# One layer's side work on fixed points: VectorE's long pieces cut and spread, GpSimd's routing first, half of a zero-clearing in the opening

## What is computed

```python
x = x + 0.5 * _L0_ffn_ref(_layernorm(x, axis=-1), ...)      # chain 1
x = x + _L0_attn_ref(_layernorm(x, axis=-1), ...)           # 16 heads of 16 channels
x = x + 0.5 * _L0_ffn_ref(_layernorm(x, axis=-1), ...)      # chain 2
x = x + 0.5 * _L1_ffn_ref(_layernorm(x, axis=-1), ...)      # 32 experts, 4 per token
x = x + _L1_attn_ref(_layernorm(x, axis=-1), ...)
x = x + 0.5 * _L1_ffn_ref(_layernorm(x, axis=-1), ...)
```

## Time and profile before

| | us |
|---|---|
| median of 3 runs | 1552.89 |
| lowest and highest | 1550.59, 1554.79 |
| profiled execution, its own time | 1556.93 |
| its span, first to last instruction | 1555.1 |
| first layer's maxima and scores, first to last start (L389, L400) | 71.6 to 504.3 |

### The profile page before, as it was taken

The page is one execution under the profiler, slowest core; times in us unless marked ns, Lnnn a source line. Parts: engine busy times, 40 slices in busy tenths (PEclk is TensorE's granted clock), DMA queues, the critical chain, the costliest instruction groups (busy, mean ns, idle before and its releaser), DMA issues.

```text
span 1555.1 us, 20966 instructions
## 1 busy us (share of the span) xinstructions
PE 1224.5 (79%) x5960; PEld 751.6 (48%) x5960; DVE 935.5 (60%) x2702; ACT 676.1 (43%) x1706; POOL 547.7 (35%) x558
## 2 busy tenths in 40 slices
PE   4777877887878528999556989889989999299990
PEld 2432333332232316888423546555655656188870
DVE  6777566856754312232359887988788695232227
ACT  2223544554647114555324554455355354155550
POOL 2053270246353134555121121144125133455550
PEclk8786897998989759999779999999999999699995
DMA  4657065092031345554301000020001001444448
GB/s 117 109 93 205 21 88 177 21 164 101 26 138 39 125 165 190 164 160 149 133 13 42 28 28 1 1 79 31 1 11 45 33 33 44 149 160 156 156 136 274
DMA packets 80379, 147.94 MB, mean 95 GB/s; under 512 B 13885, under 2 KB 62078, under 8 KB 77326
## 3 DMA queue, kind: packets, MB, share of 16 engines
q1 hardware_dynamic: 62286, 104.41, 24.0%
q0 software_dynamic: 17408, 42.00, 7.6%
q10 hardware_dynamic: 576, 0.18, 0.0%
HBM read 83.21 MB, written 63.00 MB: 94 GB/s over the span
## 4 chain that ended last, share of the span: by engine, by line
PE 53%; DVE 28%; issue 7%; ACT 6%; DMA 2%; POOL 2%; SPq 1%; another core or an unknown queue 1%; DVEq 0%; POOLq 0%; ACTq 0%
PE m_psG L1057 11%; PE m_psY L1073 5%; DVE a_t L1483 4%; PE a_psO L414 3%; DVE a_mx L758 3%; PE a_psA L1251 3%; PE a_psU L389 3%; DVE a_nb L1491 3%; PE a_psS L400 3%; PE m_psX L1048 3%; PE a_psU L1233 2%; PE a_psT L310 2%; PE a_psU L1239 2%; PE a_psO L1274 2%; ACT a_pr L1354 2%
## 5 line engine op out<-in xcount | busy, mean ns | idle before, releaser
L138 POOL DMA_INDIRECT outs_dram<-m_ys,dest x192 | 184.0, 958 | 165.7 <-ACT m_ys L996 152.8
L1354 ACT ACTIVATE a_pr<-a_psA,a_nb 128x512 f32<-128x512 f32 (+3 forms) x256 | 132.6, 524 | 220.4 <-DVE a_nb L1491 219.5
L758 DVE TENSOR_REDUCE a_mx<-a_psU 128x1 f32<-128x512 f32 x256 | 165.2, 684 | 104.8 <-PE a_psU L389 91.0
L1016 DVE TENSOR_TENSOR m_hm<-m_psG,m_sg 128x128 f32<-128x128 f32 x192 | 55.9, 291 | 282.7 <-ACT m_sg L990 173.6
L1410 POOL TENSOR_TENSOR a_q<-a_q,a_t 64x512 f32<-64x512 f32 x64 | 80.8, 1263 | 358.0 <-DVEq L1486 336.2
L1057 PE MATMUL m_psG<-arena,m_xgT 128*128 x768 | 205.6, 391 | 0.8 <-issue 0.2
L533 ACT ACTIVATE a_P<-a_psS 128x512 f32<-128x512 f32 x256 | 143.6, 597 | 93.6 <-PE a_psS L400 80.2
L138 POOL DMA_INDIRECT rows_dram<-a_xd,slot x128 | 124.7, 974 | 142.5 <-DVE a_xd L124 76.2
L389 PE MATMUL a_psU<-arena 96*128 96x512 bf16 x256 | 108.0, 428 | 45.8 <-DVE a_mx L758 35.3
L1057 PEld LDWEIGHTS m_psG<-arena,m_xgT 128*128 128x128 f32 x768 | 133.5, 194 | 16.1 <-issue 4.0
L1491 DVE TENSOR_REDUCE a_nb<-a_psA 128x1 f32<-128x512 f32 (+3 forms) x256 | 113.2, 484 | 36.8 <-PE a_psA L1253 27.1
(11 more groups left out here) (249 smaller groups left out, 2222.7 us busy)
## 6 DMA issues: line engine op xcount, KB each, us to landing
m_xg<-rows_dram SPq DMA_DIRECT2D x48, 512.0 KB
arena<-in_mo_w SPq DMA_DIRECT2D x9, 2048.0 KB
arena<-part_dram SPq DMA_DIRECT2D x96, 128.0 KB
rows_dram<-arena SPq DMA_DIRECT2D x12, 1024.0 KB, 12.1
arena<-outs_dram SPq DMA_DIRECT2D x16, 512.0 KB, 3.6
part_dram<-a_part SPq DMA_DIRECT2D x16, 384.0 KB
m_xg<-outs_dram SPq DMA_DIRECT2D x8, 512.0 KB, 4.4
m_ys<-outs_dram SPq DMA_DIRECT2D x8, 512.0 KB, 5.0
```

The source lines that it names most:

```text
L138: pool.indirect_dma_start(out=rows_dram, out_offset=bass.IndirectOffsetOnAxis(ap=slot[:, c:c + 1], axis=0), in_=row, in_offset=None).then_ ...
L758: dve.tensor_reduce(mx[g % 2][:, 4 * kt + qt:4 * kt + qt + 1], psU[n % 2][:, :], AX, ALU.max).then_inc(u_free, 1)
L1354: ins = act.activation(pr[S % 2][:, AT[t]:AT[t] + (t + 1) * P], psA[:, AT[t]:AT[t] + (t + 1) * P], ACT.Exp, bias=nb[S % 2][:, t:t + 1], sc ...
```

## The change

- The places are new: `F1` 7 to 20, `F2` 25 to 33 (that is point 1 of the iteration after), scales of the projections at 7 and 11 instead of 0, their rows, transposes and products at 13 to 18 instead of 1 to 8.
- A chain has 19 steps instead of 13: one `gate_row` per point, `gates` in two halves (`GA`, `GB`), and in chain 2 the scales in two pieces (`SB`, `SE`).
- `batch_scales` is cut into `scales_begin` (10 instructions) and `scales_end` (6), at `QSC`, `OSC` and `SB`/`SE`.
- The two additions of the output projection stand at one point.
- `bases` moves behind the first two reductions of iteration 0; `places` from point 0 to point 3 of iteration 1.
- POOL: per iteration `bias`, then all of the routing or the table writes, then `terms`, then all rows.
- Six of the twelve zeroing DMAs are issued in the opening, from a part of the probabilities' buffer (`blank`) that POOL clears first; ACT's first exponential waits for them. The other six stay in iteration 0, and none are left in iteration 1.

```diff
-    F1, F2 = 7, 25
-    QSC, QLN, QT, QK, QV = 0, 1, 2, 3, 7
-    AT, OP, OA, OST, OSC = 19, 20, 21, 23, 24
+    F1, F2 = 20, 33
+    TX, GM, GAP, GA, GB, TH, LM, LA, ST, SB, SE, XD = 1, (2, 3, 4, 5), 6, 7, 8, 9, 10, 11, {1: 12, 2: 13}, 14, 16, 18
+    QSC, QLN, QT, QK, QV = (7, 11), 13, 14, 15, 17
+    AT, OP, OA, OST, OSC = 19, 20, 21, 23, (29, 30)
...
+def scales_end(dve, link, sc):
+
+    root_steps(dve, link, sc.var[:, :], sc.rstd[:, :], sc.tmp[:, :], 2)
...
-    inverse_root(dve, link, sc.var[:, :], sc.rstd[:, :], sc.tmp[:, :])
+    root_guess(dve, link, sc.var[:, :], sc.rstd[:, :], sc.tmp[:, :])
+    root_steps(dve, link, sc.var[:, :], sc.rstd[:, :], sc.tmp[:, :], 1)
...
+                        if st == 0 and c == 0:
+                            act.wait_ge(wiped[0], 16 * 6)
...
-                if i == -1 and p == F1 + 12:
+                if i == 0 and p == 0:
                     dve.tensor_scalar(weight[:, :], weight[:, :], 0.5, None, ALU.mult)
                     bases()
-                if i == 1 and p == 0:
+                if i == 1 and p == 3:
                     places()
...
+            pool.memset(blank, 0.0).then_inc(blanked, 1)
...
-            for i in range(-2, B + 2):
+            for i in range(0, B + 2):
                 b = i + 1
-                if 1 <= b < B:
+                if i == 0:
+                    pool.wait_ge(rest_in, 16 * NREST)
+                if i < B:
+                    bias(i)
+                if i == 0:
+                    for part_of in range(3):
+                        route(part_of)
+                if 1 <= i <= 3:
+                    entry((0, 22, 43)[i - 1], (22, 43, 64)[i - 1])
+                if b < B:
                     for c in range(4):
                         terms(b, c)
...
+                if 0 <= i - 2 < B:
+                    rows(i - 2, 0, TPB * TOPK)
...
+            sp.wait_ge(blanked, 1)
+            clear(0, blank)
```

More of the change, by code:

```diff
@@ L183, in turn_units @@
         out = []
-        if ffn_at(i, p, 1):
-            out += [("x",) + ffn_at(i, p, 1) + (u,) for u in range(2)]
-        if ffn_at(i, p, 7):
-            out.append(("h",) + ffn_at(i, p, 7))
+        if ffn_at(i, p, TX):
+            out += [("x",) + ffn_at(i, p, TX) + (u,) for u in range(2)]
+        if ffn_at(i, p, TH):
+            out.append(("h",) + ffn_at(i, p, TH))
         if p == QT and 0 <= i + 1 < B:
@@ L200, in main_units @@
         out = []
-        for step, js in ((2, (0, 1)), (3, (2,)), (4, (3,))):
+        for j, step in enumerate(GM):
             if ffn_at(i, p, step):
-                out += [("m",) + ffn_at(i, p, step) + (j,) for j in js]
-        if ffn_at(i, p, 8):
-            out += [("l",) + ffn_at(i, p, 8) + (c,) for c in range(2)]
+                out.append(("m",) + ffn_at(i, p, step) + (j,))
+        if ffn_at(i, p, LM):
+            out += [("l",) + ffn_at(i, p, LM) + (c,) for c in range(2)]
         if QK <= p < QK + 4 and 0 <= i + 1 < B:
@@ L261, in first_layer @@
         mrest, mterm, identb = sb("mrest", [P, 16]), sb("mterm", [P, TPB * NR], BF16), sb("identb", [P, P], BF16)
-        stripes = Pr[0:3, 0:4 * L].bitcast(BF16)[:, 0:7 * L]
+        stripes, blank = Pr[0:3, 0:4 * L].bitcast(BF16)[:, 0:7 * L], Pr[:, 4 * L:8 * L]
+        blanked, wiped = sem("blanked"), [sem(f"wiped{i}") for i in range(2)]
         Osb, AO, rec = sb("Osb", [P, L]), sb("AO", [P, TPB * D]), sb("rec", [P, 16])
@@ L670, in side @@
                     dve.tensor_copy(identb[:, :], ident[:, :])
-                if i == -2 and p == F1 + 7:
+                if i == -2 and p == F1 + TH:
                     dve.wait_ge(rows_in, 16)
@@ L738, in side @@
                 if 0 <= b < B:
-                    if p in (OA, OA + 1):
+                    if p == OA:
                         dve.wait_ge(biased, TPB * (b + 1))
-                        add(("p", b, p - OA), b, p - OA)
+                        for u in range(2):
+                            add(("p", b, u), b, u)
                     if p == OST:
@@ L815, in rows @@
                 if b == 0 and lo == 0:
-                    pool.wait_ge(rows_clear, 16 * 12)
+                    for n in range(2):
+                        pool.wait_ge(wiped[n], 16 * 6)
                 for n in range(lo, hi):
@@ L853, in _, with clear @@
                              ).then_inc(pads_in, 16)
-            def clear(lo, hi):
-                w = zero.shape[1]
+            def clear(half, source):
+                w = source.shape[1]
                 rows = rows_dram.rearrange("(p j) d -> p (j d)", p=P)
-                for n in range(lo, hi):
-                    sp.dma_start(rows[:, n * w:(n + 1) * w], zero).then_inc(rows_clear, 16)
+                for n in range(6 * half, 6 * half + 6):
+                    sp.dma_start(rows[:, n * w:(n + 1) * w], source).then_inc(wiped[half], 16)
+            sp.wait_ge(blanked, 1)
+            clear(0, blank)
             for i in range(-2, B + 2):
```

103 lines of the change are left out of this document (54 added, 49 removed).

## The result

| | before | after |
|---|---|---|
| median of 4 runs, us | 1553.14 | 1588.68 |
| lowest to highest | 1550.59 to 1554.79 | 1585.02 to 1591.15 |
| profiled execution, its own time; span | 1556.93; 1555.1 | 1590.43; 1588.6 |

The change is slower: the ratio is 1.0228, with an interval of 1.0201 to 1.0255. The forecast was 1535 with a range of 1510 to 1562.

A forecast was written before the change was run, and what follows sets the result against it. Neither PE nor DVE alone was taken to bound the kernel, but their handover of two buffers; -3 - 9 - 6 = -18 on 1556.9 us gave 1538.9, and 4.0 lower for the median, 1535; range 1510 to 1562.

The forecast's parts named there:

- What I cost at nothing: Opening clear, clears gone from iteration 1, table writes before `terms`, batch 2's rows and the tail: each given no time.
- `entry` before `terms`: POOL's 22 indirect DMAs take 28 us from point 3 on; `terms` may start 5 us late, covered, so no cost.
- Term A: Iteration 0: 26 maxima in a row, then the remaining PE work, 90.0 us against 92.6: -3, between -7 and +5.
- Term B: Iterations 1 to 4: cutting DVE's side work into pieces shortens PE's waits for reductions: -9, between -3 and -14.
- term C: PE's lower clock behind long waits: less throttled time once waits shrink, -6, between 0 and -12.
- signs named for B and C: Iteration 1 on: no 3 us PE wait for a reduction, such waits under 15 us; clock above 0.90 in iterations 1-3.
- Terms five us late: `terms` may start 5 us late behind the table writes; first use is 17 points off, over 60 us: no cost.
- the clears: Clear in the opening: nothing, up to 5 us if still running; clears gone from iteration 1: nothing, bound -6.6.
- the tail: After the loop, 42.9 us, one batch's chain in latency, stays: 0, between -1 and +3.
- One sign of being wrong: Iteration 0: first maxima later than 72 us would show the prediction wrong.
- The second half too dense: Rival: points 13 to 25 of iterations 1 to 3 cost 0.6 us more each, +22, giving 1563 us; chance 0.14.

The follow-up runs named there:

- e1: The kernel after, with POOL waiting for the landing after every fourth indirect DMA (but for the last batch's rows): 1513.08 us, ratio 0.9761.
- e5: The kernel before, with POOL waiting for the landing after every fourth indirect DMA of a portion (not of the last batch): 1531.75 us, ratio 0.9914.
- e8: The kernel after, with six clearings of a small tile after every fourth indirect DMA and no wait for a landing: 1525.10 us, ratio 0.9841.
- e2: The kernel before, with POOL's portions joined into one run of 16 rows and one of 22 or 21 table writes: 1622.82 us, ratio 1.0467.
- e10: The kernel after, with one clearing of a small tile after every indirect DMA and no wait for a landing: 1521.92 us, ratio 0.9816.
- e9: The kernel after, with POOL waiting for the landing after every eighth indirect DMA: 1548.06 us, ratio 1.0007.

## Why the prediction was wrong

**The step that failed** is the one headed "What I cost at nothing", at "`entry` before `terms`". It counted the 22 indirect DMAs as 28 us of POOL's own time and asked who waits for POOL. The time was right (26.8 + 0.96 us from 174.0) and the question too narrow. Joined in one run these DMAs make PE's signals to VectorE and ScalarE late, from about the eighth on. Nobody waits for POOL there. The same holds for the 16 rows of a batch, which the change also joined and the text spoke of only for the tail. By the comparison of e1 with the kernel after this is worth 70.5 us of the loop.

**The evidence was there.** The earlier trace rows show ScalarE standing 6.59 us for something no record ends. The text noted PE's 6.5 us beside it and gave nothing for it, as it began before the clears. It was the largest late signal in the kernel before, behind its entries of 8, 7 and 7; the next held a reduction up for 2.15 us. An idle that several engines share and that nothing ends is a question to answer before a sum is made.

**Term A** (-3, between -7 and +5) held: 90.8 us against a forecast of 90.0, in part by luck. The 27th maximum starts at 104.11, so the first part took 31.7 us where the sum had 28.4, and the rest 59.1 where it had 61.6. The collisions came as described: in iteration 0, VectorE beside POOL's routing,

```profile
91.19 0.83 DVE L137 TENSOR_SCALAR a_sa_var<-a_sa_mv 128x4 f32<-128x4 f32 x1
92.26 2.28 DVE L58 TENSOR_SCALAR a_sa_rstd<-a_sa_tmp 128x4 int32<-128x4 int32 x1
94.77 1.20 DVE L65 TENSOR_TENSOR a_sa_tmp<-a_sa_tmp,a_sa_var 128x4 f32<-128x4 f32 x1
```

and PE stood 5.41 us behind them, where the sum had 4 for all collisions. Two of the three rows are instructions with one input in SBUF. The Trainium skill, "SBUF — State Buffer", section "Who interferes with whom", says that such an instruction "does not contend with GpSimd" outside the modes that use both ports; whether these ran in such a mode no row shows.

**Term B** (-9) and **term C** (-6) can be judged only where no signal is late. There the change's own gain is 19 to 24 us against the 18 of the sum. The cuts gave 4.6 of it by the medians (not separated from nothing), where the prediction had 6.5 + 1 for the same cuts. Of the signs named for B and C two held in e1 from iteration 1 on: no PE wait of 3 us for a reduction (longest 1.9), and the granted clock above 0.90 (0.95, 0.95, 0.98). The kernel after had 0.81, 0.88 and 0.86. The clock rose in the loop from 0.90 (e5) to 0.92 (e1) and PE's busy time fell by 3.8 us, against the 6 of term C. The mechanism of term C also worked the other way, and by more: 22.0 of the 70.5 us that the long runs cost were PE's longer busy time at the lower clock.

**Terms five us late.** Right about the delay, wrong about the cover. The text looked at the first use of the terms, 17 points off. The nearer limit is the two buffers of `qf`: PE stood 3.81 us in e1 and 12.83 in e8. In the kernel after it has no such wait above 1.5 us, so this was no part of the loss.

**The rest that was costed at nothing** stood: the clears, and the tail (handover 72.5 us against 70.9). One sign of being wrong did come, the first maximum at 75.33 us where 72 was the limit. It cost nothing, as the first reduction starts at 76.2 against 76.4.

**The sums.** The forecast's own range is misadded: the upper ends of the three terms, +5, -3 and 0, give +2 and not -7, so 1555 and not 1546. The 1.29 us per indirect DMA are 20.49 / 16 = 1.28 and hold a gap; in a run it is 1.27. Neither changes on which side of the range the result fell.

**The rivals.** "The second half too dense" named the right side and 1563 us, but e1 refutes its mechanism as the cause of the loss: the density is there and the loss is not. No rival had the joined runs, so the range ended 26.7 us short.

## What to carry to other kernels

Do not let GpSimd issue long runs of indirect DMAs back to back while other engines wait for TensorE's signals: a wait for the landing after every fourth makes four of them take 6.2 us instead of 5.1 and took 75 us off this kernel's time. When portions of such DMAs are joined, count the run's length as a cost for the engines that TensorE feeds, and so for TensorE, not for GpSimd. And read idle time that several engines share and no record ends first: it was 6.6 us in the profile before, and it was the largest thing in the one after.

## What the runs showed of the hardware

- At one indirect DMA per 1.27 us, PE's signals to VectorE and ScalarE come late, from about 10 us after the run's start; reductions stand up to 8.33 us for them in the kernel after (9.2 in e2). The updates by VectorE, ScalarE and POOL come within 0.013 us of their instructions in the same trace, and those of the DMAs about 2 us after issue. In the nine kernels with a late sum of 0 at most three of PE's updates in the loop are over 0.4 us late, the longest by 1.40.
- At one per 1.43 us the late sum is less than half as much (22.1 against 59.8), at 1.55 and above none. A backlog that fills above some pace between 1.43 and 1.55 us fits these rows. The runs don't tell a limit on the pace from one on the number in a row (at most four follow one another where nothing is late, and eight or more where something is), except that e10 paces single ones and e8 fours without a wait, and both are free of it.
- What fills is not shown. PE's updates come in a burst once they come: at 414.98 to 415.12 us there are five, of matmuls that ended, by the modelled ends, from 405.5 to 408.3. As the ends are modelled, a matmul that itself ended late can't be told from a signal that left late. Records go missing beside it: of the 1536 updates that the loop's 96 indirect DMAs make the trace holds 240 in the kernel after, 434 in e9, 973 in e1 and 1345 in e10. Each time here comes with a span and a clock of its own, so it seems to be of a recorded execution, and no run tells a lateness of the chip from one that the recording adds.
- It outlives the run. In the kernel after the last of 21 entries is issued at 410.53, and the longest stand ends at 415.04:

```profile
415.04 1.29 DVE L794 TENSOR_REDUCE a_mx<-a_psU 128x1 f32<-128x512 f32 x2 [8.33 <-remote]
415.00 0.59 ACT L564 COPY a_Osb<-a_psO 128x512 f32<-128x512 f32 x1 [7.13 <-remote]
```

- It is not the DMA engines' load. Between 383 and 420 us of the kernel after, their busy share in tenths (40 slices), and the queues (packets, MB, share of 16 engines), with the run of 21 entries in the second:

```profile
DMA  9999999991000000000000000000000000000000
q1 hardware_dynamic: 249, 3.56, 22.7%
q0 software_dynamic: 672, 0.01, 1.4%
```

The late reductions there are those of 398.1 to 415.0, with the DMA engines under a tenth busy. No packet of the queues that load instructions falls there, so it is not code loading either.
- The Trainium skill, "SBUF — State Buffer", section "Who interferes with whom", states that "DMA never contends with a compute engine". The sentence is about ports to SBUF, and for the data moved the rows agree. It must not be read as "indirect DMAs of GpSimd cost the compute engines nothing": PE, VectorE and ScalarE stand together in the kernel after, and cutting the runs takes 75.6 us off its median. Whether any port of SBUF has part in that no run shows.
